# Causal mask of an attention stage: TensorE accumulates it into the scores of several heads at once, GpSimd no longer selects behind the exponential

## What is computed

```python
def _L0_attn_ref(x, Wq, Wk, Wv, Wo):          # x is the layer-normed input, 16 heads of 16
    q, k, v = (proj(Wq), proj(Wk), proj(Wv))
    q = _apply_rope(q, cos, sin)
    k = _apply_rope(k, cos, sin)
    scores = jnp.einsum('bhqd,bhkd->bhqk', q.astype(jnp.float32), k.astype(jnp.float32)) / math.sqrt(dh)
    causal = jnp.tril(jnp.ones((S, S), dtype=bool))
    scores = jnp.where(causal, scores, jnp.finfo(jnp.float32).min)
    probs = jax.nn.softmax(scores, axis=-1).astype(v.dtype)
    attn = jnp.einsum('bhqk,bhkd->bhqd', probs, v)
    attn = attn.transpose(0, 2, 1, 3).reshape(B, S, D)
    return jnp.einsum('bsi,oi->bso', attn, Wo)
```

## Time and profile before

| | us |
|---|---|
| median of 3 runs | 691.93 (690.14 to 693.06) |
| the profiled execution: time | 691.5 |
| the profiled execution: span of the core | 689.6 |
| PE busy, share of the span | 552.6 (80%) |
| DVE busy | 463.2 (67%) |
| ACT busy | 366.2 (53%) |
| POOL busy | 329.9 (48%) |
| granted TensorE clock, mean | 0.935 |

### The profile page before, as it was taken

How to read it: one execution, slowest core, us unless ns; L and a number is a source line. 1 busy time by engine, 2 the same in 40 slices (tenths; PEclk the granted TensorE clock), 3 DMA queues, 4 the chain that set the end, 5 groups by cost and what they waited for, 6 DMA issues and landing times.

```text
span 689.6 us, 12671 instructions
## 1 busy us (share of the span) xinstructions
PE 552.6 (80%) x4116; PEld 419.9 (61%) x4116; DVE 463.2 (67%) x1134; ACT 366.2 (53%) x681; POOL 329.9 (48%) x342
## 2 busy tenths in 40 slices
PE   0567899898889889879889999868888999999300
PEld 0345564564556455443667888757777999999300
DVE  2786974788748983775497675516777666665288
ACT  1254489357762869038654533526667666666200
POOL 3456155025421444015253777752655677777521
PEclk9977999899998999799999999998999999999755
DMA  8996000000000000000210543645999788786692
GB/s 295 307 299 225 1 3 2 1 3 1 3 2 0 3 1 2 1 2 3 75 53 17 210 145 106 211 170 143 217 215 226 120 141 134 135 137 105 101 349 91
DMA packets 54702, 73.36 MB, mean 106 GB/s; under 512 B 4784, under 2 KB 48496, under 8 KB 54640
## 3 DMA queue, kind: packets, MB, share of 16 engines
q1 hardware_dynamic: 40192, 53.25, 25.3%
q0 software_dynamic: 14448, 19.31, 16.0%
HBM read 33.22 MB, written 39.12 MB: 105 GB/s over the span
## 4 chain that ended last, share of the span: by engine, by line
PE 26%; DVE 10%; issue 5%; ACT 4%; POOL 3%; DMA 2%; SPq 0%; DVEq 0%; POOLq 0%; ACTq 0%
PE gate_ps L1810 8%; PE y_ps L1833 6%; PE y_ps L1775 3%; POOL xs_dram L1189 3%; ACT w_all L1227 2%; PE gate_ps L882 2%; PE up_ps L882 2%; PE m_ps L1789 2%; DVE total L1644 1%; DVE total L1659 1%; PE up_ps L1821 1%; DMA added<-acc_dram 1%; DVE ystats L1646 1%; PE up_ps L1822 1%; DVE rxT_lo L1627 1%
## 5 line engine op out<-in xcount | busy, mean ns | idle before, releaser
L1201 POOL DMA_INDIRECT acc_dram<-yout,xin x79 | 121.7, 1541 | 67.1 <-ACT yout L1325 27.2
L633 DVE TENSOR_REDUCE nmax<-a_ps 128x2 f32<-128x768 f32 (+3 forms) x88 | 95.6, 1122 | 15.3 <-PE a_ps L781 14.9
L442 POOL TENSOR_SCALAR_AFFINE_SELECT probs<-probs 128x256 f32<-128x256 f32 (+1 forms) x96 | 48.4, 513 | 94.8 <-ACT probs L508 94.7
L508 ACT ACTIVATE probs<-a_ps 128x1024 f32<-128x1024 f32 (+1 forms) x96 | 81.3, 886 | 13.7 <-PE a_ps L803 12.4
L779 PE MATMUL a_ps<-KTt,QT 96*128 96x128 bf16 (+3 forms) x256 | 69.1, 342 | 18.7 <-DVE nmax L633 10.5
L1189 POOL DMA_INDIRECT xs_dram<-xrow,idx x64 | 66.4, 1038 | 29.6 <-issue 18.0
L1810 PE MATMUL gate_ps<-w_all,rxT_hi 128*128 x316 | 78.8, 331 | 1.3 <-DVE rxT_lo L1627 1.3
L409 POOL TENSOR_TENSOR rot<-rot,rest 128x512 f32<-128x512 f32 x16 | 21.9, 1369 | 86.0 <-DVE rest L605 86.0
L1833 PE MATMUL y_ps<-w_all,hT_hi 128*128 x237 | 57.3, 310 | 4.2 <-DVE hT_lo L1632 4.2
L779 PEld LDWEIGHTS a_ps<-KTt,QT 96*128 96x128 bf16 x256 | 26.8, 105 | 49.7 <-DVE nmax L633 27.2
L803 PE MATMUL a_ps<-QT,KTt 99*128 99x512 bf16 (+3 forms) x256 | 49.4, 302 | 7.2 <-DMA QT<-nT 3.0
(11 more groups left out here) (264 smaller groups left out, 1480.3 us busy)
## 6 DMA issues: line engine op xcount, KB each, us to landing
xs_dram<-zeros SPq DMA_DIRECT2D x1, 10783.5 KB, 38.6
xin<-xs_dram SPq DMA_DIRECT2D x79, 136.5 KB, 2.9
stage<-in_wex_dram SPq DMA_DIRECT2D x16, 608.0 KB, 5.2
acc_dram<-zeros SPq DMA_DIRECT2D x2, 2176.0 KB, 16.7
added<-acc_dram SPq DMA_DIRECT2D x8, 512.0 KB, 7.7
x_all<-in_x_dram SPq DMA_DIRECT2D x4, 512.0 KB, 6.7
acc_dram<-yst SPq DMA_DIRECT2D x4, 512.0 KB, 2.9
total<-acc_dram SPq DMA_DIRECT2D x4, 512.0 KB, 7.2
```

The source lines that it names most:

```text
L442: pool.affine_select(out=pr, in_=pr, pattern=[[0, nh], [1, P]], compare_op=ALU.is_ge, fill=0.0, base=0, channel_multiplier=-1).then_inc(ma ...
L508: nc.scalar.activation(dst, src, ACT.Exp, scale=float(DH) ** -0.5).then_inc(a_act, 1)
L633: nc.vector.tensor_reduce(nmax[:, i, h:h + nh].rearrange("p (b h) -> p b h", h=hb), src, AX.X, ALU.max, negate=True).then_inc(a_dve, 1)
L1201: pool.indirect_dma_start(out=acc[a][:, :], out_offset=bass.IndirectOffsetOnAxis(ap=xin[:, p % XIN, XROW - 1:XROW].bitcast(mybir.dt.uint32 ...
```

## The change

The function `diagonals` is new. It adds the mask to n heads of one PSUM bank by one matmul: the output is a pattern of n blocks of 128 columns that lie w apart, and the right operand is repeated n times.

```diff
--- before.py
+++ after.py
@@ GpSimd
-                elif kind == "score":
-                    q, u = item[1:]
-
-                    j, h0, nh = SCU[u]
-                    pool.wait_ge(a_act, seg.at("aA", item))
-                    w = S - j * P
-                    pr = probs[:, (q * len(SCU) + u) % 4, 0:nh * w].rearrange("p (h n) -> p h n", h=nh)[:, :, 0:P]
-                    pool.affine_select(out=pr, in_=pr, pattern=[[0, nh], [1, P]], compare_op=ALU.is_ge,
-                                       fill=0.0, base=0, channel_multiplier=-1).then_inc(masked, 1)
@@ TensorE
+            def diagonals(r, nh, w, per, first, left, right):
+
+                for b in range(0, nh, per):
+                    n = min(per, nh - b)
+                    to = a_ps[:, r, b // per, 0:n * w].rearrange("p (h k) -> p h k", h=n)[:, :, first:first + P]
+                    ins = nc.tensor.matmul(to, left, right.unsqueeze(1).to_broadcast([P, n, P]), start=False, stop=True,
+                                           skip_group_check=True)
+                return ins
...
                         nc.tensor.matmul(a_ps[:, r, n // hb, o:o + w], QT[0:SR, a % 2, h, i * P:(i + 1) * P],
-                                         KTt[0:SR, a % 2, h, 0:w], start=True, stop=False, skip_group_check=True)
-                        ins = nc.tensor.matmul(a_ps[:, r, n // hb, o + w - P:o + w], ident16[:], causal[:],
-                                               start=False, stop=True, skip_group_check=True)
+                                         KTt[0:SR, a % 2, h, 0:w], start=o == 0, stop=False, skip_group_check=True)
+                    ins = diagonals(r, nh, w, hb, w - P, ident16[:], causal[:])
...
                         ins = nc.tensor.matmul(a_ps[:, r, bank, o:o + w], KTt[0:QR, a % 2, h, j * P:(j + 1) * P],
-                                               QT[0:QR, a % 2, h, j * P:S], start=True, stop=True)
+                                               QT[0:QR, a % 2, h, j * P:S], start=o == 0, stop=False,
+                                               skip_group_check=True)
+                    ins = diagonals(r, nh, w, 1 if j < 2 else 512 // w, 0, causal[:], ident16[:])
...
-                    pe.wait_ge(masked, (a * QUAD + q) * len(SCU) + SC_LAST[j] + 1)
+                    pe.wait_ge(a_act, seg.at("aA", ("score", q, SC_LAST[j])))
```

More of the change, by code:

```diff
@@ L284, in attention_block @@
         nrows_in = [sem(f"nrows_in{g}") for g in range(2)]
-        masked = sem("masked")
         pv_done = sem("pv_done")
```

## The result

The changed kernel takes 696.23 us (median of 22 runs, 692.71 to 698.22), the kernel before 692.99 in 22 runs on the same chip. The ratio is 1.0043 with a 95% interval of 1.0025 to 1.0061: about 3 us slower, inside the range and 1.0 us under the forecast of 697.2. The difference lies just under the 0.5% (3.5 us) that was named as the bound of what can be told from no change, so "slower" rests on the interval of these 22 runs and on the traces. The profiled execution took 695.61 us, 4.1 more than that of before, its span 693.9, 4.3 more.

The account below looks back on a forecast made before the run. TensorE was taken as the fullest engine where scores are made, ScalarE next. A 2.8, B and C 0.8 together and D 2.1 made 5.7 us on the profiled 691.5: forecast 697.2 us, range 695.4 to 700.

Parts of the forecast that it names:

- A: First of four segments before 339 us: TensorE runs with hardly a gap, no removable mask wait; +2.8 us, 66 to 68.8.
- D: Last of the four segments, up to 339 us: ScalarE starves for TensorE, so new masks land on the path; +2.1 us.
- Rival 3: Mask matmuls in the max pass: their number, not their columns, is the price, saving 4.8 us; 692.4 us, chance 0.05.
- first term: In A up to 106 us: score units on TensorE's path pay their new masks in full; 1.6 us.
- the next two: In A: 0.5 us from 106.30 to 115, where ScalarE sets the pace; 0.7 from 115 on, where TensorE leads.
- B and C: The two middle segments: vanished mask waits nearly offset new matmuls on TensorE; +0.4 us each, 75.0 to 75.4.
- place one: In B and C, pv waits for masks queued behind GpSimd's split: 1.16 us returned against 1.0 added, net 0.
- place two: Later in B and C, pv waits for masks behind a split: 1.0 us returned, masks before pv take 0.4.
- the term before the third quad: In D from 312 us to 318.37: new masks of score units on the path; 0.79 us.
- Rival 2: Same time: more is covered, A shows 1.0 us, B and C come out even, D 1.3; 693.8 us, chance 0.27.
- Rival 1: Faster: in B and C mask waits return 2.2 us each, VectorE's L681 may help by 4.6; 687.1 us, chance 0.10.
- Rival 4: Slower by much: each score unit pays, later hand-overs pass it on, 11.6 us; 703.1 us, chance 0.08.

Follow-up runs that it names:

- e2: Changed kernel without its masks in the score pass, GpSimd's selections gone too; 687.14 us, ratio 0.9908 to the kernel before.
- e5: Kernel before with only GpSimd's work in B and C reordered, parts of splits behind masks, TensorE untouched; 690.03 us against 692.65, ratio 0.9951.
- e1: Kernel before with only the max pass's masks merged (176 matmuls instead of 256), GpSimd's selections kept; 692.4 us against 691.96, ratio 1.0009.
- e10: Changed kernel with one mask matmul for each head in both passes (256 instead of 176), same columns; 723.12 us, ratio 1.0074 to the kernel before.
- e3: Changed kernel with GpSimd's selections and pv's wait for them put back, beside TensorE's masks; 697.03 us, ratio 1.0058 to the kernel before.
- e11: Changed kernel run once more, nothing altered; 722.47 us against 717.75 for the kernel before, ratio 1.0055.
- e4: Changed kernel with every mask matmul of the score pass issued twice; 705.75 us, ratio 1.0176 to the kernel before.
- e6: Changed kernel with two unread 512-column matmuls behind each of the first ten max units of a segment; 693.02 us against 692.65 for the kernel before, ratio 1.0005.
- e7: Kernel before with e5's GpSimd order and e6's unread matmuls together; 688.5 us, ratio 0.9927 to the kernel before.
- e8: e7 plus two unread matmuls behind each of nine max units of D's second half; 713.53 us against 718.04 for the kernel before, ratio 0.9924.
- e9: e8 with one unread matmul for each of these max units instead of two; 712.64 us, ratio 0.9928 to the kernel before.
- e12: e9's kernel run again, on one chip with the changed kernel; 712.38 us, ratio 0.9927 to the kernel before.

## Why the prediction held, point by point

**Sign and size.** Forecast +5.7 against the profiled execution, measured +4.1 there, +3.2 between the medians and +3.0 by the ratio. The score parts, free of the lower clock, say +4.8. That 697.2 came within 1.0 us is in part luck: it was built on 691.5, and the kernel before has a median of 692.99 in 22 runs. The sign and the path held; the size was too large by 0.9 us against the score parts and by 2.5 against the medians.

**The removed waits.** I put the removable time at the array's wait, at most 4.4 us, and not at the weight loads' 10.4. e2 gave 3.85, hardly anything of it in A and D. Both places were put too high (0.8 for 1.16 and 0.9 for 1.0), and 0.3 us came between them, where I had nothing. GpSimd's rotations, which I counted at nothing as well, come 1.7 us earlier in the score part of C in e2 (15.78 us against 17.44); e5 shows that such a delay can reach TensorE.

**The added work.** 14.6 us of TensorE, priced by columns, held; TensorE's busy time rose by 8.2 us only: merging the max masks alone took 9.9 off (542.7 in e1), and the masks in the score pass put 18.1 on. A shown duration holds the drain and the clock, so these figures price nothing; the distances between starts do. Rival 3 (number of matmuls) fell in e1 and e10.

**A: +2.8 forecast, +2.17 behind the first exponential.** The step that failed in size is its first term, 1.6 us up to 106 us. It measured 1.04; the next two, 0.5 and 0.7, measured 0.48 and 0.65. I had counted each unit on TensorE's path in full. The rows behind it, TensorE before and after:

```profile
105.66 1.04 PE L803 MATMUL a_ps<-QT,KTt 99*128 99x512 bf16 x4 [0.29 <-DMA QT<-nT]
```

```profile
107.35 0.85 PE L820 MATMUL att_ps<-probs,V 128*32 128x384 f32 x8
108.13 0.61 PE L801 MATMUL a_ps<-QT,KTt 99*128 99x512 bf16 x2
```

The first unit of the third quad had waited 0.29 us for the maxima's DMA. Now TensorE arrives with 1.28 us of new work behind it and the wait is gone: it starts 0.93 late. Some 0.2 us more went earlier, in a wait of a max unit for its slot. The length of A in the trace, 68.90, agrees with the forecast 68.8 for the wrong reason: 1.5 of its 3.6 us came from the front, with 10.2 us of lower clock for 3.4.

**B and C: +0.4 each, measured 0.49 and 0.53.** pv at place one comes 36.72 and 37.63 us into C, 36.89 and 37.70 before: no earlier but for the front's 0.2, as said. At place two it comes 57.31 us in, 58.04 before: 0.7 earlier, 0.5 without the front's part, for 0.6. The split of the two effects is shown by e2 and e3: the masks alone cost 1.2 us, and the lost wait gives 0.67 back, at place two only.

**D: +2.1, measured 1.57 (e11: 1.56).** Term by term 0.45, 0.79, 0.50, 0.30; measured 0.45, 0.39, 0.44, 0.30. Again the term before the third quad is the one mis-sized, and again TensorE had stood there for that DMA. Before, and after, without a wait:

```profile
317.73 1.04 PE L803 MATMUL a_ps<-QT,KTt 99*128 99x512 bf16 x4 [0.24 <-DMA QT<-nT]
```

```profile
320.17 0.85 PE L820 MATMUL att_ps<-probs,V 128*32 128x384 f32 x8
321.00 0.59 PE L801 MATMUL a_ps<-QT,KTt 99*128 99x512 bf16 x2
```

Two short waits for slots before it (0.17 and 0.27 us, now 0.11 and 0.21) took 0.1 more. D's length then fell by 0.4 us where I forecast +2.1, because its front had no lower clock (25.27 for 27.25).

**Rivals.** Rival 2, "more is covered", had +2.3. It is nearer to the +3.2 of the medians than the forecast is, and further from the +4.8 of the score parts. Its sign, A growing by less than 1.5, did not come, even behind the first exponential (2.17); it named A, where 0.6 was covered, but not the place. Rival 1 fell, though its mechanism for VectorE is real:

```profile
L671 DVE SCALAR_TENSOR_TENSOR x_all<-mix,mrs,x_all x12: 472/477/895, 159.3 to 304.7; 128x256 f32<-128x256 f32 x12
```

This is e2, min, median and max in ns; the changed kernel has 473, 481 and 899, where the earlier trace rows had a median of 854. The median overstates it: the twelve take 7.39 us together in e2 and 8.67 before, so 1.3 us went with GpSimd's selections and not 12 x 0.38. Four of them still take 892 to 895 ns in e2, each beside one of GpSimd's splits; those beside nothing take 472 to 477. The prediction's second rule from the Trainium skill ("SBUF — State Buffer", section "Who interferes with whom": two SBUF inputs on VectorE contend with GpSimd reading SBUF) would have it so, and this trace agrees. It shortened nothing in A and D, where the score parts of e2 are those of before within 0.06 us; for B and C its share in e2's 1.9 us is not separated. Rival 4 fell: even e4's second copy landed at 77%.

**The clock.** I had allowed 1 us for a shift of the lower level. In single segments it moved 2.0 us (D) and 1.5 (A), in the sum 0.7, since they went opposite ways. The difference of 1.6 us between the masks' 4.8 and the 3.2 of the medians is not settled. In e11's 12 runs the changed kernel had a mean granted clock of 0.9274 and the kernel before, in 22, 0.9238. Within each of these sets the time falls by 3.0 and 4.4 us for 0.01 of mean clock, so as an estimate the difference is worth 1.1 to 1.6 us, the size that is missing. But why the clock should be higher is not shown: a busier TensorE is not enough as a reason, since e2, without the masks, had 0.941 beside 0.937.

## What to carry to other kernels

A wait that ends on GpSimd may be a matter of its queue's order: putting the masks ahead of a split that nobody needed yet gave 2.8 us in the score parts (3.4 by the ratio) with no work moved, while moving the masks to TensorE, the fullest engine, cost 3. Before adding work to the leading engine, list the places where it stands still (for a DMA, a slot, another engine): what is added ahead of such a place is free up to that wait, what comes behind costs nearly in full, and a removed wait and the added work may claim the same idle time, so that their effects don't add. Cut a noisy kernel's trace at an event that separates the stretch led by the clock from the stretch that was edited, and compare the parts.

## What the runs showed of the hardware

- In the max units, where TensorE waits for VectorE, the clock's lower level came in stretches of 3.4, 6.8 or 10.2 us (13.7 in D once), or not at all, in executions of one and the same kernel. In B and C 6.8 us of it cost 1.45 (24.66 against 23.20), in D 10.2 us cost 2.0. With TensorE's idle time filled by unread matmuls it came in none of the 20 fronts of e6, e7, e8, e9 and e12; without them in 23 of 36.
- It can also come later: 26 to 33 us into D in e1 and e7, where the score part then took 36.7 us for 34.2.
- A mask matmul whose right operand is repeated over several heads costs what its columns cost: 0.11 us at 256 and 0.22 at 512.
- One DMA of the maxima, in e1, kept TensorE waiting 2.5 us where the wait is 0.7 otherwise; it shows as 0.7 us in one segment.
- VectorE's L681 (two inputs in SBUF, 128x256; L671 in the changed kernel and e2) takes 472 to 482 ns alone and 848 to 899 where GpSimd's selections or splits run beside it for about 0.6 us or more.
